# A 16-sequence diffusion-transformer kernel: another hand-written order of its steps, and a wait added to the values' product

## What is computed

```
mod = silu(c) @ W_mod + b_mod
shift_a, scale_a, gate_a, shift_m, scale_m, gate_m = split(mod, 6)
h = _ln(x) * (1 + scale_a) + shift_a
q, k, v = split(h @ W_qkv + b_qkv, 3)
x = x + gate_a * (attend(q, k, v) @ W_proj + b_proj)
q = _ln(x) @ W_qc + b_qc
k, v = split(_ln(context) @ W_kvc + b_kvc, 2)
x = x + attend(q, k, v) @ W_cproj + b_cproj
h = gelu((_ln(x) * (1 + scale_m) + shift_m) @ W_mlp1 + b_mlp1)
x = x + gate_m * (h @ W_mlp2 + b_mlp2)
...
# layer 1
q = ada_ln(x, c) @ Wq + bq
k, v = split(ada_ln(context, c) @ Wkv + bkv, 2)
x = x + attend(q, k, v) @ Wp + bp
```

## Time and profile before

| | us |
|---|---|
| runs (3): lowest, median, highest | 2456.67, 2457.8, 2457.94 |
| the profiled execution, its time | 2459.47 |
| its span in the profile | 2457.7 |
| TensorE busy | 2394.8 (97%) |
| VectorE, ScalarE, GpSimd busy | 1875.6, 1263.5, 466.9 |
| mean granted TensorE clock | 0.993 of full speed |

### The profile page before, as it was taken

One profiled execution on the slowest core, in us unless ns is written; L12 is line 12 of the kernel. 1 busy time (PEld: TensorE's weight loads), 2 busy tenths in 40 slices (PEclk: granted clock), 3 DMA queues, 4 the chain that ended last, 5 costly groups with the idle time before them and its releaser, 6 DMA issues.

```text
span 2457.7 us, 93436 instructions
## 1 busy us (share of the span) xinstructions
PE 2394.8 (97%) x41326; PEld 1616.7 (66%) x41326; DVE 1875.6 (76%) x3532; ACT 1263.5 (51%) x1810; POOL 466.9 (19%) x510
## 2 busy tenths in 40 slices
...
GB/s 214 133 113 61 99 86 78 78 88 85 80 84 84 91 93 76 93 89 72 70 88 60 85 78 55 88 88 70 94 108 60 106 70 76 100 60 89 85 40 39
DMA packets 143669, 209.27 MB, mean 85 GB/s; under 512 B 14978, under 2 KB 75588, under 8 KB 143268
## 3 DMA queue, kind: packets, MB, share of 16 engines
...
## 4 chain that ended last, share of the span: by engine, by line
PE 91%; DVE 5%; issue 1%; ACT 1%; DMA 1%; SPq 0%; POOL 0%; POOLq 0%; DVEq 0%; ACTq 0%
PE ring L1220 38%; PE ring L1216 13%; PE o_acc L1380 12%; PE score L1327 11%; PE score L1349 9%; PE ring L1174 4%; PE score L1354 3%; DVE row_max_F L1008 3%; DVE row_max_G L1008 2%; ACT probs L1147 1%; DMA gate_now_P<-gate_rows 0%; SPq L693 0%; PE ring L1256 0%; DMA q_F<-q_parts 0%; DMA k_G<-k_parts 0%
## 5 line engine op out<-in xcount | busy, mean ns | idle before, releaser
L1147 ACT ACTIVATE probs<-score 120x2048 f32<-120x2048 f32 (+1 forms) x320 | 601.6, 1880 | 302.2 <-PE score L1354 273.5
L1008 DVE TENSOR_REDUCE row_max_F<-score 128x8 f32<-128x2048 f32 x192 | 438.6, 2285 | 88.8 <-PE score L1327 86.2
L1158 ACT ACTIVATE h_t<-ring,cols 128x256 f32<-128x256 f32 x384 | 160.6, 470 | 415.5 <-PE ring L1220 289.3
L1008 DVE TENSOR_REDUCE row_max_G<-score 128x16 f32<-128x1920 f32 x128 | 276.2, 2158 | 65.4 <-PE score L1327 65.4
L1220 PE MATMUL ring<-x_t_E,w_fc 128*32 128x256 f32 x4736 | 279.6, 380 | 0.0
L1030 DVE STREAM_TRANSPOSE o_turned<-o_acc 128x512 f32<-128x512 f32 x224 | 159.4, 712 | 127.7 <-PE o_acc L1380 127.2
L1220 PE MATMUL ring<-w_fc,h_t 128*32 128x256 f32 x3680 | 215.4, 380 | 0.0
L1220 PEld LDWEIGHTS ring<-x_t_E,w_fc 128*32 128x32 f32 x4736 | 149.0, 110 | 100.2
L1380 PE MATMUL o_acc<-probs,v_self 128*17 128x256 f32 x3072 | 203.8, 383 | 0.4 <-DVE o_turned L1030 0.4
L817 POOL TENSOR_TENSOR x<-x,gated 128x512 f32<-128x512 f32 x48 | 61.2, 1274 | 612.1 <-DVE gated L1049 611.8
L1349 PE MATMUL score<-q_F,k_F 32*128 32x256 f32 x3072 | 166.1, 302 | 9.0 <-ACT probs L1147 4.5
...
## 6 DMA issues: line engine op xcount, KB each, us to landing
...
q_G<-q_parts SPq DMA_DIRECT2D x128, 256.0 KB, 2.6
k_G<-k_parts SPq DMA_DIRECT2D x256, 120.0 KB, 2.1
...
```

Source lines behind the costliest of these rows:

```text
L1008: nc.vector.tensor_reduce(dst, src, AX.X, ALU.max).then_inc(row_max_ready[r].sem, 1)
L1147: nc.scalar.activation(probs[v % 2][0:keys, :, :], score[0:keys, :].rearrange("p (h q) -> p h q", h=2 * GROUPS), ACT.Exp, scale=SCALE).the ...
L1158: last = nc.scalar.activation(h_t[:, c, :], ps[:, c % 2 * NT:(c % 2 + 1) * NT], ACT.Gelu_apprx_tanh, bias=col(m, "fc1", c))
```

## The change

In `START`, `WITH_L1`, `TURN` and `TAIL` the same words stand in another order. Two waits are added, so that `V` may stand in front of `Q` and `K`: ScalarE's filling of `x_t_P` waits for the last `Q`, `K` and `V` of the job before, and `V` on TensorE waits for `x_t_P`. Of the tables the diff is cut to the rows that the prediction speaks of.

```diff
 TURN = """
...
-G.T1 R.LN F.O0 P.ST E.F21b e.LN c.AC E.F21b.d p.A
-F.T2 E.gld G.PV0 R.KV G.O0 R.KV.d G.O1 G.PV1
-F.T3 P.ld R.Q R.Q.d F.PV2 R.RES
+G.T1 p.A R.RES E.F21b e.A R.LN P.ST c.AC
+F.T2 F.O0 R.A G.PV0 R.KV G.PV1
+F.T3 E.F21b.d R.Q G.O0 P.gld e.LN G.O1 R.KV.d F.PV2 P.RES R.Q.d
 """.split()
 WITH_L1 = """
...
-F.S3 E.RES F.X 1R.LN 1p.NC A.PR
-1G.S1 A.PR.d B.PR E.F20a B.PR.d 1G.X
+1G.S1 1R.LN 1G.X B.PR
+F.S3 B.PR.d A.PR F.X E.F20a A.PR.d
...
@@ -1082,6 +1079,8 @@
                         act.wait_ge(mods_turned, LAYERS)
 
                     if r == "P":
+                        q_psum[r].wait_before(act, m, n)
+                        k_psum.wait_before(act, m, n)
                         v_psum.wait_before(act, m, n)
                     elif r == "R":
                         q_psum[r].wait_before(act, m, n, len(x_t[r]))
@@ -1291,6 +1290,7 @@
                 elif step == "V":
                     if n == 0:
                         pe.wait_ge(w_v_loaded, full_done(m))
+                    pe.wait_ge(x_t_ready[r].sem, x_t_ready[r].after(m, n))
                     for t in range(TT):
                         for k in range(KC):
                             last = product(ps[:, t * D:(t + 1) * D], buffer(x_t, r, m, n)[:, k, t * P:(t + 1) * P],
```

More of the change, by code:

```diff
@@ L49 @@
 TURN = """
-F.S0 f.O1 f.PV3 E.H0
+F.S0 f.PV3 f.O1 E.H0
 F.S1 E.H1 P.V
[L52 to L58, removed]
-G.T1 R.LN F.O0 P.ST E.F21b e.LN c.AC E.F21b.d p.A
-F.T2 E.gld G.PV0 R.KV G.O0 R.KV.d G.O1 G.PV1
-F.T3 P.ld R.Q R.Q.d F.PV2 R.RES
+F.S2 P.V.d E.H2 P.LN
+F.S3 A.PR F.X A.PR.d E.H3
+G.S0 F.M R.C P.K p.N
+G.S1 G.X P.ld P.K.d P.Q B.PR
```

136 lines of the change are left out of this document (68 added, 68 removed).

## The result

The changed kernel takes **2483.05 us** (median of 5 runs, 2480.82 to 2483.88) against 2457.8 for the kernel before on the same chip (5 runs): a ratio of **1.0101**, with a 95% interval of 1.0088 to 1.0115. I had forecast 2459.8 with a range to 2470. The profiled execution took 2483.88, its span is 2482.1.

The account below looks back on a forecast made before the run. TensorE's steps and layout changes, busy 2394.8 of 2457.7 us, were taken to bound the kernel, VectorE and ScalarE the start. Terms 0 + 6.0 + 0 - 3.8 - 0.2 = +2.0 us on the median 2457.8 gave 2459.8 us, range 2450 to 2470.

Parts of the forecast that it names:

- The two waits, 0: Waits on ScalarE's fill and TensorE's `V`: already satisfied by the order of steps, so they cost 0 us.
- `TURN`, +6.0: 25 turns: 0.39 less behind `G.T1`, 0.63 more behind `F.T3` from layouts, 0.24 us a turn, +6.0 us.
- `WITH_L1`, 0 us with 0.6 allowed: 19 turns: `1G.S1` and `F.S3` exchanged still sum to 7.77, other moves swap gaps of like cost; 0 us.
- the 2.08 for a product before a score step: `WITH_L1`, new `1G.S1` gap: TensorE's product in front of a score step priced at 2.08 us.
- the slower rival: VectorE queue in `TURN`: norm stretched by GpSimd's addition makes `R.LN` wait for `x_hat_R`; 2467 to 2473 us, chance 0.17.
- The condition I had named against it: `TURN`: GpSimd's next addition, `R.RES`, itself waits for `x_hat_R`, an argument against the VectorE queue; no size given.
- `START` and turns 3 to 5, -3.8: Start of the kernel: -0.9 up to turn 3, -4.7 in turn 3, about +1.8 in turn 4; sum -3.8 us.
- Turn 3, forecast at 43.5: Turn 3, before 48.24 us: would be near 43.5 us with less low clock.
- the -0.5 up to the first `F0.S0`: `START`: queries sent earlier, and `P1.K` and `P1.Q` done while the keys are on their way; -0.5 us.
- the +1.4 for the late `F0.M`: Before turn 3: `F0.M` right behind `F0.S3` waits for that step's maximum before the first `T`; +1.4 us.
- My third rival: Start gives nothing: clock falls as before, late `F0.M` eats the rest, `TURN` costs 6.0; 2463.6 to 2465 us, chance 0.13.
- `TAIL`, -0.2: `TAIL`: same steps, layouts priced alike within 0.2; -0.2 us, with +-2 for other waits.

Follow-up runs that it names:

- experiment 7: The kernel before with the two added waits alone, tables as they were: 2455.79 us, ratio 0.9993.
- experiment 2: The changed kernel with GpSimd's bias additions `1R.RES` and `R.RES` both moved to just behind `p.N` in `WITH_L1`: 2465.01 us, ratio 1.0025.
- experiment 3: The changed kernel with only the bias addition `1R.RES` moved to behind `p.N` in `WITH_L1`, `R.RES` left in place: 2467.76 us, ratio 1.0035.
- experiment 5: The changed kernel with `e.LN` in `TURN` moved back behind `R.LN` in the gap of `G.T1`: 2477.8 us, ratio 1.008.
- experiment 11: The changed kernel with `START`'s `P1.Q`, `P1.V` behind `F0.S0`, `F0.S1`, and `F0.M`, `F0.T0` behind `F1.S1`: 2476.06 us, ratio 1.008.
- experiment 10: The changed kernel with only `F0.M` and `F0.T0` of `START` moved back behind `F1.S1`: 2481.67 us, ratio 1.0097.

## Why the prediction was wrong, by its own steps

*The two waits, 0:* right (experiment 7). `V` stands behind `Q` and `K`, and the waits ask for what is long true.

*`TURN`, +6.0:* right in place and size. The gap behind `F.T3` is 4.27 (1485.45 to 1489.72) and that behind `G.T1` 3.26 (1477.75 to 1481.01), as priced:

```profile
1485.45 0.30 PEld L1349 LDWEIGHTS score<-q_F,k_F 32*128 32x128 f32 x8 [0.42 <-ACT probs L1146]
...
1486.37 1.59 PEld L1215 LDWEIGHTS ring<-x_t_R,w_q 128*128 128x128 f32 x8
1487.98 0.57 PEld L1173 LDWEIGHTS ring<-ident,x_hat_E 128*128 128x128 f32 x4
1488.73 0.56 PEld L1380 LDWEIGHTS o_acc<-probs,v_self 128*17 128x17 f32 x16 [0.17 <-issue]
1489.72 0.42 PEld L1327 LDWEIGHTS score<-k_F,q_F 32*128 32x128 f32 x12 [0.42 <-issue]
```

The transposes in front of `PV` cost 0.75 (1487.98 to 1488.73), the `PV` behind them 0.99. Both estimates held: four transposes cost 0.75 in front of column tiles and 0.39 in front of more whole-array work. That agrees with the rule of the Trainium skill (TensorEngine Tiling (Array Packing), Key Properties) that had been set against the edit, that a change of tiling mode drains TensorE. Moving the one word back took 0.19 of the 0.23 away.

***`WITH_L1`, 0 us with 0.6 allowed: this is the step that failed.*** The part of it that I did lay out, `1G.S1` and `F.S3` exchanged, came to 7.64 (`1G.S1` at 762.41 to `G.S0` at 770.05) against 7.77 before: a small gain, 0.13, which turn 20 and experiment 2 show pure. The term that I had too high is the 2.08 for a product before a score step: in the earlier trace rows it holds a wait for `row_max_F`, and here the product took 1.94 (763.84 to 765.78). But I compared TensorE's gaps alone and dismissed the rest as an exchange "between gaps of like cost". On VectorE and GpSimd the table puts `1p.A` in front of `G.O1` and both bias additions right behind `1p.N`, and the 0.73 that the earlier trace rows has for `x_hat_R` is from a moment at which GpSimd was idle. In its place the runs showed 2.59 us for `x_hat_R`, and a wait of 1.16 us for TensorE in each of 15 turns, 17.4 us; with the additions out of the way the kernel took 18.0 us less. The mechanism was in the prediction, as the slower rival, with its price of a stretched norm read from the earlier trace rows. I looked for it in `TURN` only, where it did not come (`x_hat_R` took 0.70 and `R.LN` did not wait), and not in the table with the most GpSimd work. The condition I had named against it, that `R.RES` waits for the `x_hat_R` of its own job, protects a job from itself; it does not keep the additions of *other* jobs away. The Trainium skill (SBUF — State Buffer, Who interferes with whom) says that the pair of ports is an exclusive lock and the later operation stands until the first is done. The numbers agree with one waiting for the other: each instruction of the norm that met an addition took 1.30 to 1.37 us instead of 0.41 (experiment 3), and the addition takes 1.29. But each of them ended 0.15 to 0.16 us behind its addition (800.79 + 1.29 is 802.08, 800.93 + 1.30 is 802.23), sooner than the 0.41 of a whole instruction; what passes in between, the trace does not tell.

*`START` and turns 3 to 5, -3.8:* wrong in sign, the second step that failed. The spans say +4.4 up to turn 6, the median +5.4 for `START`. The good halves came: VectorE no longer stands 4.19 us for the gate's rows as in the earlier trace rows, and `B0.PR` in the empty gap shortened the stretch from `F.S3` to `G1.S0` from 8.22 to 4.02 (141.92 to 145.94), where I had 3.77. In the changed kernel, VectorE's use of the gate, and the windows of turn 3 up to `G1.S0` and of the 8 us behind it:

```profile
87.57 0.69 DVE L1046 TENSOR_TENSOR gated<-ring,gate_now_P 128x512 f32<-128x512 f32 x1
```

```profile
132.39:145.94 13.55, 10.26 (x162) 6.75 (x158) 13.11 (x17) 1.28 (x3) 0.11 (x1) 1.00 0.27 87
145.94:154.00 8.06, 5.95 (x74) 4.99 (x75) 6.35 (x10) 0.38 (x1) 1.26 (x1) 0.79 0.01 2
```

The low clock is gone from where I saw it and comes later in the turn: 0.79 in the second window, 0.86 in the rest of the turn (154.00 to 178.12). (The kernel before had a second low stretch too, 0.51 from 158.0 to 164.9.) Turn 3, forecast at 43.5, took 45.73. In experiment 2 it took 43.39, and in experiment 5, with the same `START` and `WITH_L1`, 44.04, so part of the 45.73 is chance. The terms that failed are the -0.5 up to the first `F0.S0`, where the spans differ by +1.6, and in turns 0 to 2 the +1.4 for the late `F0.M`: these turns came to +3.4 instead of -0.4. I priced `P1.Q` by where it went, had no term for `P1.V`, and did not price the gaps they left: two scores with nothing behind them. My third rival named these score steps, but allowed the start only to give nothing, not to cost. Experiment 11 shows that the two edits together give the cost back. How it divides between them (experiment 10 alone shows nothing clear), and between the plain waits and the low clock, is not separated.

*`TAIL`, -0.2:* the spans say -1.1. The kernel before with only the waits added had 130.0 for this stretch where the kernel before had 130.6, so some 0.6 of it is chance.
